# Cross attention of a decoder layer on one core: values by stationary compressed values, sums from ScalarE's exponentials

## The reference, cut to what matters

```python
x = x + xattn(layernorm(x), ctx_2048, itok, W_kvc, W_dq, W_uq, W_qr, W_uk, W_kr, W_uv, W_o)
x = x + attn(layernorm(x), Wq, Wk, Wv, Wo)
x = x + ffn(layernorm(x), w_router, wg, wu, wd, sg, su, sd)      # 8 experts, top 2, and 2 shared

def xattn(q, kv, seg_id, ...):             # q: 16 x 64 x 256; kv: 16 x 1601 x 256
    kv_c = kv @ W_kvc                      # compressed keys and values, 64 wide
    q_c = q @ W_dq                         # 96 wide
    q_nope, q_rope = ...                   # 16 heads
    k_nope, v, k_rope = kv_c @ W_uk, kv_c @ W_uv, rope(kv_c @ W_kr)
    scores = (q_nope @ k_nope.T + rope(q_rope) @ k_rope.T) / sqrt(128 + 64)
    good = (k_ids <= seg_id) & (k_ids >= seg_id - 8)
    attn = softmax(where(good, scores, -1e30))
    return (attn @ v).reshape(b, lq, H * HD) @ W_o
```

## Time and profile before

| | us |
|---|---|
| median of 3 runs | 550.16 |
| lowest, highest | 545.77, 550.23 |
| profiled execution, whole | 551.02 |
| its span in the trace | 549.2 |
| the stretch from the first scores of tile 0 to the end of the last projection (30.61 to 197.14 of the span) | 166.53 |

### The profile page before, as it was taken

How to read it: one execution, slowest core, us unless ns; L and a number is a source line. 1 busy time by engine, 2 the same in 40 slices (tenths; PEclk the granted TensorE clock), 3 DMA queues, 4 the chain that set the end, 5 groups by cost and what they waited for, 6 DMA issues and landing times.

```text
span 549.2 us, 11518 instructions
## 1 busy us (share of the span) xinstructions
PE 522.8 (95%) x4452; PEld 393.9 (72%) x4452; DVE 261.6 (48%) x558; ACT 157.8 (29%) x298; POOL 59.4 (11%) x70
## 2 busy tenths in 40 slices
PE   7969999999999989999689999899999999999997
PEld 6667887887787877887478888555555555556886
DVE  3637767767767527898654222122222222222234
ACT  1234444444444314444321111121122212221111
POOL 2000000000000002212200550000000000000560
PEclk9789999999999999999979999999999999999999
DMA  9600000000396049000070316278777877782241
GB/s 297 275 0 21 20 1 19 19 0 19 104 391 289 1 179 399 4 1 0 1 289 4 113 67 219 94 254 314 275 270 281 314 279 268 280 306 70 73 129 38
DMA packets 24457, 82.06 MB, mean 149 GB/s; under 512 B 2881, under 2 KB 16513, under 8 KB 20322
## 3 DMA queue, kind: packets, MB, share of 16 engines
q1 hardware_dynamic: 21536, 75.93, 37.8%
q0 software_dynamic: 1536, 4.20, 2.5%
q10 hardware_dynamic: 1346, 1.38, 0.8%
HBM read 73.11 MB, written 8.39 MB: 148 GB/s over the span
## 4 chain that ended last, share of the span: by engine, by line
PE 86%; DVE 6%; issue 3%; DMA 2%; ACT 2%; POOL 0%; DVEq 0%; ACTq 0%; POOLq 0%
PE ps L1646 16%; PE ps L1612 13%; PE ps L1216 10%; PE ps L1670 8%; PE ps L1624 6%; PE ps L1269 5%; PE ps L1250 5%; PE ps L1294 5%; PE ps L1282 3%; PE ps L1487 3%; DMA seg_i<-in_seg 2%; PE ps L1265 2%; PE ps L1242 1%; PE ps L1535 1%; DVE w_routed L594 1%
## 5 line engine op out<-in xcount | busy, mean ns | idle before, releaser
L1646 PE MATMUL ps<-w_routed,xnT 128*64 x320 | 93.8, 436 | 1.6 <-DVE x_sb L905 1.6
L1612 PE MATMUL ps<-xT_all,w_shared 128*128 128x256 f32 x320 | 76.9, 386 | 0.0
L1646 PEld LDWEIGHTS ps<-w_routed,xnT 128*64 128x64 f32 x320 | 42.0, 137 | 38.5 <-issue 27.2
L1612 PEld LDWEIGHTS ps<-xT_all,w_shared 128*128 128x128 f32 x320 | 61.7, 194 | 8.9 <-issue 0.4
L1216 PE MATMUL ps<-consts_a,w_routed 128*128 128x128 f32 x400 | 51.5, 275 | 6.5 <-ACT w_routed L1027 2.9
L1216 PEld LDWEIGHTS ps<-consts_a,w_routed 128*128 128x128 f32 x400 | 44.2, 141 | 13.9 <-issue 4.4
L1670 PE MATMUL ps<-w_routed,hidT 128*64 x200 | 47.4, 384 | 0.0
L1646 PE MATMUL ps<-w_shared,xnT 128*64 128x384 f32 (+1 forms) x160 | 46.9, 436 | 0.0
L1646 PE MATMUL ps<-x_up,xnT 128*64 128x384 f32 (+1 forms) x160 | 46.9, 436 | 0.0
L1185 ACT ACTIVATE sil<-ps 128x256 f32<-128x256 f32 x40 | 15.3, 383 | 84.8 <-PE ps L1612 84.8
L1175 ACT COPY hidT<-ps 128x384 f32<-128x384 f32 x20 | 9.6, 480 | 100.7 <-PE ps L1216 100.7
(11 more groups left out here) (181 smaller groups left out, 897.1 us busy)
## 6 DMA issues: line engine op xcount, KB each, us to landing
w_routed<-in_w_routed SPq DMA_DIRECT2D x8, 1920.0 KB, 14.4
x_up<-in_w_routed SPq DMA_DIRECT2D x10, 1280.0 KB, 5.9
w_shared<-in_w_routed SPq DMA_DIRECT2D x10, 1280.0 KB, 6.2
b_down<-in_w_routed SPq DMA_DIRECT2D x10, 640.0 KB, 5.4
w_shared<-in_w_routed SPq DMA_DIRECT2D x10, 640.0 KB, 5.3
w_shared<-in_w_shared SPq DMA_DIRECT2D x1, 3840.0 KB, 12.0
w_shared<-in_w_uvo SPq DMA_DIRECT2D x1, 2560.0 KB, 15.3
x_slots<-sil SPq DMA_DIRECT2D x16, 160.0 KB, 2.2
```

The source lines that it names most:

```text
L1612: last = pe.matmul(ps[:, UP_BANK[m], half_ * D:(half_ + 1) * D].rearrange("p (n t) -> p n t", n=2), w_shared[:, j, at:at + P], xT_all[:, i ...
L1646: last = pe.matmul(ps[rows, b, 0:hi - lo], xnT[:, k, rows], w, start=k == 0, stop=k == KT - 1)
```

## The change

The statistics of the softmax and the place of its division move. VectorE no longer subtracts the maximum: the keys are copied with the factor -1/sqrt(192) and the mask has the other sign, so that PSUM holds negated scores; VectorE takes the minimum of each row and head, and ScalarE's exponentials read PSUM directly with scale -1, that minimum as a bias per partition, and the sum as a second output. For that there is one exponential for each row group, 8 of 128 elements a b, in place of one of 1024. VectorE then takes the reciprocals of the sums and multiplies the 1024 probabilities of SBUF by them (`divided`), ahead of the transposes. TensorE multiplies with the compressed values stationary (64 columns) and the transposed probabilities moving, 512 columns for each of the two heads of the row groups, into the lower and the upper 64 partitions of one bank: what comes out is already transposed, so `values_T` and its 4 transposes go away. The orders of the three engines are changed too.

```diff
@@ -178,6 +178,8 @@
         qr_t = cut(H, R)
         QT = cut(TB, H, LQ)
         nmx = sb("nmx", [P, TB, NP_])
+        neg_top = sb("neg_top", [P, TB, NP_])
+        sums = sb("sums", [P, TB, NP_])
         Pb = cut(TB, NP_, P)
         PT = cut(TB, NP_, P)
         rec = sb("rec", [P, TB, NP_])
@@ -594,23 +596,18 @@
                 dve.tensor_copy(QT[:, :, 0:8, :].rearrange("p b h q -> p h b q"),
                                 ps[:, 0:2, :].rearrange("p n (h b q) -> p (n h) b q", b=TB, q=LQ)).then_inc(qt_lo, 1)
-            def softmax_in(i, b, link_):
+            def maxima(i, b):
                 s = scores_at(b)
-                dve.wait_ge(s_ps, 2 * TB * i + 2 * b + 1)
-                dve.tensor_reduce(nmx[:, b, 0:4], s[:, 0:4], AX.X, ALU.max)
-                dve.wait_ge(s_ps, 2 * TB * i + 2 * b + 2)
-                link_(dve.tensor_reduce(nmx[:, b, 4:8], s[:, 4:8], AX.X, ALU.max))
-
-                dve.tensor_tensor(Pb[:, b], s, nmx[:, b, :].unsqueeze(2).to_broadcast([P, NP_, P]),
-                                  ALU.subtract).then_inc(sub_done, 1)
-
-            def values_out(i, b, link_):
-                u = values_at(b)
-                dve.wait_ge(u_ps, TB * i + b + 1)
-                link_(dve.reciprocal(rec[:, b, :].rearrange("p (b h) -> p b h", b=2), u[:, :, :, KVC]))
-                dve.tensor_tensor(Un[:, b].rearrange("p (b h) c -> p b h c", b=2), u[:, :, :, 0:KVC],
-                                  rec[:, b, :].rearrange("p (b h) -> p b h", b=2).unsqueeze(3).to_broadcast([P, 2, 4, KVC]),
-                                  ALU.mult).then_inc(un_done, 1)
+                for g in range(2):
+                    n = slice(4 * g, 4 * g + 4)
+                    dve.wait_ge(s_ps, 2 * TB * i + 2 * b + g + 1)
+                    dve.tensor_reduce(neg_top[:, b, n], s[:, n], AX.X, ALU.min).then_inc(top_ready, 1)
+
+            def divided(i, b, link_):
+                dve.wait_ge(exp_done, TB * i + b + 1)
+                link_(dve.reciprocal(rec[:, b, :], sums[:, b, :]))
+                dve.tensor_tensor(Pb[:, b], Pb[:, b], rec[:, b, :].unsqueeze(2).to_broadcast([P, NP_, P]),
+                                  ALU.mult).then_inc(p_done, 1)
             def residual(i, link_):
                 dve.wait_ge(proj_ps, i + 1)
@@ -619,16 +616,16 @@
             def body(i, link_, ahead, behind, more):
                 if ahead:
                     normed(i + 1, 2 * i + 1 if not isinstance(i, int) or i > 0 else 2, xn, xT_ps, xn_ready, i + 1)
-                softmax_in(i, 0, link_)
+                maxima(i, 0)
+                divided(i, 0, link_)
                 if behind:
                     residual(i - 1, link_)
-                softmax_in(i, 1, link_)
+                maxima(i, 1)
                 if ahead:
                     front_k(i + 1, link_)
-                values_out(i, 0, link_)
+                divided(i, 1, link_)
                 if ahead:
                     front_q(i + 1)
-                values_out(i, 1, link_)
                 if more:
                     link_(dve.bn_stats(bn[:], x_sb[:, i + 2, :]))
                 if ahead:
@@ -645,7 +642,7 @@
             link(dve.tensor_tensor(dist, keypos[:].unsqueeze(1).to_broadcast([P, NT, P]),
                                    seg[:].unsqueeze(2).to_broadcast([P, NT, P]), ALU.subtract))
             link(dve.tensor_tensor(dist, dist, dist, ALU.mult))
-            dve.tensor_scalar(win[:], dist, (LOOKBACK / 2) ** 2, NEG, ALU.is_gt, ALU.mult).then_inc(win_ready, 1)
+            dve.tensor_scalar(win[:], dist, (LOOKBACK / 2) ** 2, -NEG, ALU.is_gt, ALU.mult).then_inc(win_ready, 1)
             dve.wait_ge(row_in, 16)
@@ -662,7 +659,7 @@
             dve.wait_ge(x_in, 16)
             body(0, link, True, False, True)
             base = steps[0]
-            K = 10
+            K = 8
             with dve.Fori(1, NT - 2) as i:
                 n = [0]
@@ -1012,19 +1009,26 @@
                 act.copy(Qtok[:, :, 0:KVC], lat_at()).then_inc(qlat, 1)
             def k_out(i):
-                after(act, u_ps, TB * i)
+                act.wait_ge(kT_ps, i + 1)
+                act.activation(KTb[:], kT_at(), ACT.Copy, scale=-XSCALE).then_inc(kT_done, 1)
+
+            def kv_out(i):
+                after(act, ut_ps, TB * i)
                 act.wait_ge(kv_raw, i + 1)
                 act.copy(kv_ext[:, :, 0:KVC], Ktok[:, :, 0:KVC]).then_inc(kvx, 1)
-                act.wait_ge(kT_ps, i + 1)
-                act.copy(KTb[:], kT_at()).then_inc(kT_done, 1)
             def qt_hi_out(i):
                 act.wait_ge(qt_hi_ps, i + 1)
                 act.copy(QT[:, :, 8:16, :].rearrange("p b h q -> p h b q"), qT_at(2)).then_inc(qt_hi, 1)
             def exps(i, b):
-                act.wait_ge(sub_done, TB * i + b + 1)
-                act.activation(Pb[:, b], Pb[:, b], ACT.Exp, scale=XSCALE).then_inc(p_done, 1)
+                s = ps[:, 4 + 2 * b:6 + 2 * b, :].rearrange("p r (h t) -> p (r h) t", t=P)
+                for g in range(2):
+                    act.wait_ge(top_ready, 2 * TB * i + 2 * b + g + 1)
+                    for n in range(4 * g, 4 * g + 4):
+                        last = act.activation(Pb[:, b, n, :], s[:, n, :], ACT.Exp, scale=-1.0,
+                                              bias=neg_top[:, b, n:n + 1], accum_out=sums[:, b, n:n + 1])
+                last.then_inc(exp_done, 1)
             def pt_out(i, b):
                 act.wait_ge(pt_ps, TB * i + b + 1)
@@ -1038,18 +1042,19 @@
                 exps(i, 0)
                 if ahead:
                     xT_out(i + 1)
+                    qc_kv_out(i + 1)
                 pt_out(i, 0)
-                if ahead:
-                    qc_kv_out(i + 1)
                 exps(i, 1)
                 ut_out(i, 0)
+                if ahead:
+                    lat_out(i + 1)
                 pt_out(i, 1)
                 if ahead:
-                    lat_out(i + 1)
                     k_out(i + 1)
                 ut_out(i, 1)
                 if ahead:
                     qt_hi_out(i + 1)
+                    kv_out(i + 1)
             xT_out(0)
             qc_kv_out(0)
@@ -1058,6 +1063,7 @@
             act.copy(w_m[:].rearrange("p j d -> p (j d)"), ps[:, 4:8, :].rearrange("p b n -> p (b n)")).then_inc(absorb_m, 1)
             k_out(0)
             qt_hi_out(0)
+            kv_out(0)
             body(0, True)
             with act.Fori(1, NT - 1) as i:
                 body(i, True)
@@ -1283,6 +1289,12 @@
                                          start=True, stop=True)
                 return last
+            def valuesT_work(b):
+                for h in range(2):
+                    last = pe.matmul(ps[KVC * h:KVC * h + KVC, 4 + 2 * b, :].rearrange("p (j t) -> p j t", t=P), kv_ext[:, b, 0:KVC],
+                                     PT[:, b].rearrange("p (j h) t -> p j h t", h=2)[:, :, h, :], start=True, stop=True)
+                return last
+
             def uT_work(b):
                 for j in range(NP_ // 2):
                     last = transpose(ps[:, 4 + 2 * b, j * P:(j + 1) * P], Un[:, b, 2 * j:2 * j + 2, :])
@@ -1348,11 +1360,7 @@
             def values(i, b):
                 pe.wait_ge(pt_done, TB * i + b + 1)
                 pe.wait_ge(kvx, i + 1)
-                values_work(b).then_inc(u_ps, 1)
-
-            def values_T(i, b):
-                pe.wait_ge(un_done, TB * i + b + 1)
-                uT_work(b).then_inc(ut_ps, 1)
+                valuesT_work(b).then_inc(ut_ps, 1)
             def project(i):
                 pe.wait_ge(ut_done, TB * i + TB)
@@ -1364,30 +1372,27 @@
                     project(i - 1)
                 if ahead:
                     xT(i + 1)
+                    kv(i + 1)
+                    qc(i + 1)
                 probs_T(i, 0)
                 scores(i, 1)
-                if ahead:
-                    qc(i + 1)
-                    kv(i + 1)
-                values(i, 0)
                 if ahead:
                     y_rope(i + 1)
                 else:
                     keep_busy(7)
-                values_T(i, 0)
+                values(i, 0)
+                if ahead:
+                    y_lat(i + 1)
+                else:
+                    keep_busy(6)
                 probs_T(i, 1)
                 if ahead:
-                    y_lat(i + 1)
+                    k_T(i + 1)
                 else:
                     keep_busy(4)
                 values(i, 1)
                 if ahead:
-                    k_T(i + 1)
                     q_T(i + 1, 0, qt_lo_ps)
-                else:
-                    keep_busy(4)
-                values_T(i, 1)
-                if ahead:
                     q_T(i + 1, 1, qt_hi_ps)
```

(4 more changed lines are left out.)

## The result

| | before | changed |
|---|---|---|
| median, us | 550.09 (6 runs) | 554.61 (6 runs) |
| lowest, highest | 545.77, 550.24 | 553.56, 556.15 |
| profiled execution, its span | 551.02, 549.2 | 553.95, 552.1 |
| first scores to the last projection's end | 166.5 | 168.8 (32.31 to 201.08) |

The ratio is 1.0084, 95% interval [1.0051, 1.0116]: 0.8% slower, inside the 1% that counted as no change in the prediction, and clear of noise. The forecast was 553.0 in 545 to 563. Between the two profiled spans (2.9 us) the start is 1.7 longer, the stretch of tiles 2.2 longer, and all that comes behind it 1.0 shorter (351.0 us for 352.1).

A forecast was written before the change was run, and what follows sets the result against it. TensorE's queue of work was taken to bound each tile; with 1.14 us removed, two chains stay as long. Tile terms +2.25, +0.74, -0.9 and +0.2 summed to +2.3, giving 553 us, range 545 to 563.

The forecast's parts named there:

- the 1.14 of the sum: TensorE's work in a tile: values and values_T removed, new matmuls added, 3.04 - 1.90 = 1.14 us less.
- The tiles' sum: All tiles together: +2.25 for tiles 1 to 5, +0.74 tile 6, -0.9 tile 0, +0.2 tile 7, sum +2.3 us.
- p: Pitch of ScalarE's 128-element exponentials with bias and sum, start to start: taken as 0.38 us, expected from 0.30 to 0.43.
- chain A: From scores to next scores through second exponentials, divided, rotation, q_T and lower queries' copy: 17.93 + 8p, 20.97 us a tile.
- chain B: From scores to next scores through y_lat, ScalarE's two copies and values, without exponentials: 20.6 us, longest below p = 0.34.
- The wait before the scores: TensorE before the next scores: idle for 0.5 to 0.7 us, released by the lower queries' copy (L594).
- probs_T of b = 0 hidden: TensorE reaches the first probs_T at 7.32 us; the product is ready at 6.69, hidden up to p = 0.46.
- Values in 0.95, side by side: TensorE's values call: its two matmuls run together on halves of 64 columns, 0.95 us against 1.82 serially.
- rival 2: In values: the halves run one after the other, 1.82 us each, +1.8 a tile, 562 in all; chance 0.11.
- Tile 0's clock: After tile 0's wait for the exponential: 1.65 us lost to TensorE's lower clock; half taken, 21.15 against 22.01, -0.9.
- Rival 1: ScalarE between minima and divided: exponentials cost more, 558 us at p = 0.46, 568 at 0.54; chance 0.27.
- Rival 3: TensorE stays the bound and is faster: 19.4 us a tile, about 541 in all; chance 0.16.

The follow-up runs named there:

- e1: The changed kernel with exponentials that hand out no sum, the division dividing by one: 552.81 us, ratio to the kernel before 1.0026.
- e5: The changed kernel with both halves of values on the same 64 partitions, so they run one after the other: 568.56 us, ratio to the kernel before 1.0320.
- e7: The changed kernel reordered, second scores ahead of the first probs_T, with the lower queries' copy divided between VectorE and ScalarE: 541.21 us, ratio to before 0.9819.
- e6: The kernel before with only the minimum and the short exponentials from PSUM, no sum, old values and orders: 549.54 us, ratio 0.9955.
- e2: The changed kernel with TensorE and ScalarE in the order of the kernel before: 576.65 us, ratio to the kernel before 1.0473.

## Why the prediction was right, point by point

- **What bounds, and that the removed work would not come back as time**: right. TensorE's busy time in a tile fell from 20.16 to 19.31, and the tile grew. The fall is 0.85 and not the 1.14 of the sum: two values calls are 0.12 longer than taken, and the second probs_T, which a wait now follows, counts 1.04 in place of 0.87.
- **The tiles' sum.** Forecast +2.3, measured +2.3 (168.8 against 166.5); by parts, tiles 1 to 5 +2.25 against +3.15, tile 6 +0.74 against +0.58, tile 0 -0.9 against -1.38, tile 7 +0.2 against -0.08. The agreement of the total is better than that of its parts, and that is luck.
- **p.** Taken 0.38, measured 0.343; between the bounds 0.16 and 0.54. With the measured value chain A gives 17.93 + 2.74 = 20.67, chain B 20.66 by its own terms (the prediction wrote 20.6), and 21.15 was measured, 0.5 more. Along chain A the lengthenings are these: the copy of the lower queries to the scores took 0.37, not the 0.10 taken from a place outside the loop (+0.27); the way from the minimum to the product's end took 4.44, not 4.29, since the last exponential and its sum take their whole length and not only the pitch (+0.15); from q_T to that copy 1.20, not 1.07 (+0.13); and from the rotation's start to q_T 3.91, not 3.79, since q_T had to let k_T and a values call of 1.01 go ahead (+0.12). Against them stand 0.09 at the first probs_T, 0.09 by which the rotation starts before the product's end, and 0.01 in the copy. These make 0.48. So that 20.97 came near 21.15 is in part luck: p was taken 0.04 too long, 0.30 us over eight, and the other terms 0.48 too short.
- **Chain A and chain B.** Both exist. The rotation does wait behind `divided(i, 1)`, and through k_T, which the prediction named in brackets; it is 0.21 longer than chain B, as e1 shows, so each 0.01 of p counts 0.08 only down to there. The wait before the scores was forecast as 0.5 to 0.7 and is 0.82.
- **probs_T of b = 0 hidden** (7.32 forecast, 7.23 measured) and **y_rope's input long there**: right.
- **Values in 0.95, side by side**: 1.01; rival 2 would have cost 12 us and e5, which forces it, stands 13.8 above the changed kernel, 1.7 of it from tile 0's clock.
- **Tile 0's clock**: half the loss was taken, all of it went. TensorE's wait is split in 1.60 and 0.56 by qc. That the split saved the clock is not shown: e5 has the same two waits and lost 1.7 us of it. Leaving it open, as the prediction did, was right.
- **Rival 1** did not hold, since p stayed under 0.43. The Trainium skill (ScalarE: Activation LUTs, What ACT_TABLE_LOAD costs) gives constants from which 0.29 us is an estimate for a pass with a bias; e1 shows 0.26 to 0.27, from PSUM, and the measurement decides. Reading the sum adds 0.08 us to the pitch.
- **Rival 3** did not hold for this order; e7 shows that its number, 19.4 a tile, was the right one for a kernel that covers the round trips by its order and divides the copy.
- **Not foreseen**: the start. It holds about 2 of the 4.5 us, most likely, and was taken as unchanged, on one profile of before.

## What to carry to other kernels

When an edit takes work from the engine that bounds, add up the orders of all engines from one loop-carried wait to the next before crediting anything. Here 0.85 us less of TensorE's busy time bought nothing, since two round trips, the copy of the second probabilities and the copy of the lower queries, no longer had work to cover them; the product on VectorE, which holds back the rotation, added 0.2 us to that. Then ask which independent work could be moved into the waits: with the second scores, which depended on nothing new, moved forward and the other pieces placed to match, +0.8% became -1.2%, and with a divided copy -1.8%. Compare the start of the profiles too: an engine that waits for its first data may leave that wait at either clock.

## What the runs showed of the hardware

- TensorE's clock after a wait. In the start, waits of 1.41 and 1.66 us kept 1.00; waits of 1.89, 2.07, 2.19, 2.41, 2.58, 2.74, 2.75 and 2.83 were followed by 0.50 between 15 and 20 us. In tile 0 a wait of 1.74 kept it (e6), and one of 2.92 did not the earlier trace rows; two waits of 1.60 and 0.56 with the four matmuls of qc between them kept it in the changed kernel, and 1.59 and 0.56 did not in e5. In the tiles of e2 a wait of 2.03 to 2.04 lost it three times and kept it three times (windows at 0.93 and 1.00 take turns).
- An exponential of 128 elements from PSUM with a bias starts every 0.26 to 0.27 us (e1), with its sum every 0.34; the sum is a record of its own, 217 ns on the mean, which overlaps both neighbours.
- Two float32 matmuls of 64 columns and 512 moving ones take 1.01 us on the two halves of the array and 1.87 on the same half (e5).
